# Statistics, the first query eviction and the second query product ahead of a second attention, in another order

## What is computed

```python
x = x + tanh(g_xattn[0]) * L0_xattn(_layernorm(x), ctx, ...)     # cross attention
x = x + tanh(g_ffn[0])   * L0_ffn(_layernorm(x), ...)            # 8 experts, one per token, and a shared one
x = x + tanh(g_xattn[1]) * L1_xattn(_layernorm(x), ctx, ...)     # cross attention with bias and mask
x = x + tanh(g_ffn[1])   * L1_ffn(_layernorm(x), ...)            # ReLU with LoRA, two of them
```

```python
_layernorm: (x - mean) / sqrt(var + eps)
q = (query @ w_q.T + b_q) ;  scores = (q * SCALING) @ k.T + attn_bias, masked ;  softmax
```

## Time and profile before

| | us |
|---|---|
| median of 3 runs | 190.07 |
| lowest, highest | 189.88, 190.09 |
| the profiled execution | 189.79 |
| its span, first to last instruction | 188.0 |
| TensorE busy in it | 171.0 (91%) |
| VectorE busy in it | 145.8 (78%) |
| ScalarE busy in it | 79.9 (43%) |
| GpSimd busy in it | 78.4 (42%) |

### The profile page before, as it was taken

One profiled execution on the slowest core, in us unless ns is written; L12 is line 12 of the kernel. 1 busy time (PEld: TensorE's weight loads), 2 busy tenths in 40 slices (PEclk: granted clock), 3 DMA queues, 4 the chain that ended last, 5 costly groups with the idle time before them and its releaser, 6 DMA issues.

```text
span 188.0 us, 4325 instructions
## 1 busy us (share of the span) xinstructions
PE 171.0 (91%) x1606; PEld 94.8 (50%) x1606; DVE 145.8 (78%) x364; ACT 79.9 (43%) x178; POOL 78.4 (42%) x88
## 2 busy tenths in 40 slices
PE   8768599999998979899998969989999998998994
PEld 2234236555576446366665923333555555643593
DVE  0599997889989799385666496799989996869942
ACT  3253284664473342255554002245544556255300
POOL 8729991004043864005666603255674454110000
PEclk9999969999999999999999997999999999999999
DMA  6999999940002010444421030000000000000012
GB/s 158 321 420 362 257 239 247 207 137 2 3 0 24 29 58 31 89 105 91 78 51 31 6 111 4 0 2 2 3 0 3 0 3 0 3 0 0 3 40 71
DMA packets 19558, 15.01 MB, mean 80 GB/s; under 512 B 3493, under 2 KB 18087, under 8 KB 19282
## 3 DMA queue, kind: packets, MB, share of 16 engines
q1 hardware_dynamic: 18370, 13.17, 27.9%
q0 software_dynamic: 736, 1.07, 1.8%
q10 hardware_dynamic: 432, 0.50, 1.1%
HBM read 7.82 MB, written 6.85 MB: 78 GB/s over the span
## 4 chain that ended last, share of the span: by engine, by line
PE 53%; DVE 26%; issue 7%; DMA 5%; POOL 5%; ACT 2%; SPq 0%; DVEq 0%; POOLq 0%
PE bank L877 44%; PE bank L954 6%; DMA xr<-x_in 3%; POOL rstd L311 3%; DVE oT L640 2%; DVE Sa L633 2%; DVE xn L585 2%; POOL Sx L384 2%; DVE st L566 2%; PE bank L1193 2%; DVE Vx L606 2%; DVE mx L635 2%; DMA sorted_rows<-Pe,slot 1%; DVE QT L614 1%; DMA big<-sorted_rows 1%
## 5 line engine op out<-in xcount | busy, mean ns | idle before, releaser
L877 PE MATMUL bank<-Kx,QT 128*64 128x512 f32 x128 | 34.9, 629 | 2.6 <-DVE Sx L626 2.0
L311 POOL TENSOR_TENSOR rstd<-ve,nhalf 128x2 f32<-128x2 f32 x16 | 11.7, 728 | 54.1 <-DVE ve L572 54.0
L461 ACT ACTIVATE Pe<-Sx 128x512 f32<-128x512 f32 x32 | 20.2, 630 | 27.3 <-POOL Sx L384 15.1
L954 PEld LDWEIGHTS bank<-cst,Pe 128*128 128x128 f32 x128 | 13.8, 143 | 25.1 <-issue 14.6
L372 POOL DMA_INDIRECT routed_rows<-big x15 | 14.8, 984 | 19.3 <-DVE big L842 12.2
L465 ACT ACTIVATE big<-bank 128x512 f32<-128x512 f32 x32 | 18.8, 587 | 8.5 <-PE bank L954 8.2
L954 PE MATMUL bank<-cst,Pe 128*128 128x128 f32 x128 | 21.4, 291 | 0.7 <-ACT Pe L461 0.6
L384 POOL TENSOR_TENSOR Sx<-Sa,mx 128x512 f32<-128x512 f32 x16 | 16.8, 1049 | 11.3 <-DVE mx L635 11.3
L640 DVE RECIPROCAL oT<-bank 128x128 f32<-128x128 f32 x16 | 15.3, 953 | 3.7 <-PE bank L877 3.6
L877 PE MATMUL bank<-zb 128*32 128x512 bf16 x47 | 15.5, 473 | 2.5 <-DVE bo L597 1.4
L414 ACT ACTIVATE xn<-xr,nmr,rstd 128x128 f32<-128x128 f32 x20 | 9.1, 486 | 16.0 <-DVE nmr L578 16.0
(11 more groups left out here) (110 smaller groups left out, 302.9 us busy)
## 6 DMA issues: line engine op xcount, KB each, us to landing
sorted_rows<-empty SPq DMA_DIRECT2D x1, 4686.0 KB, 29.0
wgu<-rgu SPq DMA_DIRECT2D x1, 2048.0 KB, 10.6
wdn<-rdn SPq DMA_DIRECT2D x1, 1024.0 KB, 12.6
big<-sorted_rows SPq DMA_DIRECT2D x15, 66.0 KB, 1.9
ctxT<-ctx_in SPq DMA_DIRECT2D x2, 256.0 KB, 4.7
xr<-x_in SPq DMA_DIRECT2D x2, 256.0 KB, 5.3
wf<-ffn SPq DMA_DIRECT2D x1, 512.0 KB, 4.4
Kx<-KT SPq DMA_DIRECT2D x16, 32.0 KB
```

The source lines that it names most:

```text
L311: pool.tensor_tensor(rstd[:, w], ve[:, w], nhalf[:, w], ALU.pow).then_inc(s_pow, 1)
L461: act.activation(Pe[:, u % 3, :], Sx[:, u % 2, :], ACT.Exp).then_inc(s_exp, 1)
L877: return pe.matmul(o, l, r, start=first, stop=last, **k)
L954: ins = pe.transpose(bank[2 + u % 2][:, m * P:(m + 1) * P], Pe[:, u % 3, m * P:(m + 1) * P], ident)
```

## The change

Only orders change; no instruction is new except that two `keep_warm` pairs are gone.

1. VectorE, ahead of the second attention: residual and statistics of pieces 0 and 1 come first, then the normalise of piece 0, residual and statistics of piece 2, the normalise of piece 1, Q's first eviction, residual and statistics of piece 3, the normalise of piece 2.
2. TensorE: the product of Q's piece 1 no longer stands ahead of the attention but behind the scores of unit 0, and the two pairs of `keep_warm` around it are left out.

```diff
-            for a in range(PIECES):
+            def residual2(a):
+
                 dve.wait_ge(d_yg[a], 16)
                 dve.scalar_tensor_tensor(out=xres[2][:, piece(a), :], in0=yg[:, piece(a), :], scalar=tg[:, 2:3],
                                          in1=xb[:, piece(a), :], op0=ALU.mult, op1=ALU.add).then_inc(s_res, 1)
                 dve.wait_ge(s_res, RES_X2 + a + 1)
-                if a >= 1:
-                    normalise(2, a - 1)
-                if a == 3:
-                    q_evac(1, 0)
                 stats(2, a)
+
+            for a in (0, 1):
+                residual2(a)
+            normalise(2, 0)
+            residual2(2)
+            normalise(2, 1)
+            q_evac(1, 0)
+            residual2(3)
+            normalise(2, 2)
             attention(1, ffn1_step)
...
                         if bp < PAIRS:
                             scores(layer, 2 * bp + hh)
+                        if bp == 0 and hh == 0 and layer == 1:
+                            q_proj(1, 1)
...
                 xn_transpose(2, a)
-                keep_warm(6, 2)
-                q_proj(1, a)
-                keep_warm(6, 2)
+                if a == 0:
+                    keep_warm(6, 2)
+                    q_proj(1, 0)
+                    keep_warm(6, 2)
             attention(1, ffn1_up)
```

## The result

The changed kernel takes 189.22 us (median of 20 runs, 188.23 to 189.91) against 190.03 for the kernel before beside it (20 runs, 189.01 to 191.25). The ratio is 0.9957, 95% interval 0.9937 to 0.9977: 0.8 us faster, between 0.4 and 1.2.

The account below looks back on a forecast made before the run. The prediction took the chain of waits to bound the kernel, TensorE on it for 53% of the span, VectorE 26%. Unit 2's scores coming about 1.07 us sooner, lasting to the end, gave 190.07 - 1.07 = 189.0 us, range 188.3 to 189.6.

Parts of the forecast that it names:

- 1.78 us of unused time: Q's first product, ended at 117.92, waits 1.78 us for its eviction while VectorE does residual 3 and normalise 2.

Follow-up runs that it names:

- e4: Changed kernel with keep-warm matmuls filling TensorE's idle stretches at 21.9 and 109.7 us (7, and 6 + 20 in place of 16); 187.75 us, ratio 0.9892.
- e3: Kernel before with keep-warm matmuls filling TensorE's idle stretches at 21.9 and 109.7 us (7, and 6 + 20 in place of 16); 189.43 us, ratio 0.9976.
- e1: Changed kernel with VectorE's new order alone, TensorE keeping the old one; 189.43 us, ratio 0.9966.
- e2: Changed kernel with TensorE's new order alone, VectorE keeping the old one; 191.75 us, ratio 1.0087.
- e8: Changed kernel with only the idle stretch at 109.7 us filled (6 + 20 keep-warm matmuls in place of 16); 188.49 us, ratio 0.9932.
- e7: e4 without the pair of keep-warm matmuls ahead of the transposes of piece 2; 187.79 us, ratio 0.9905.
- the first filling: 7 keep-warm matmuls in TensorE's idle stretch at 21.9 us; alone on the changed kernel 187.92 us, alone on the kernel before 189.45 us.
- e6: e4 with 24 in place of 20 keep-warm matmuls ahead of the transposes of piece 0; 189.01 us, ratio 0.9952.

## What to carry to other kernels

Slack hides not only work but chance: before, 1.78 us of unused time hid where the low clock lay, and an order that uses the slack up exposes it, so an idle stretch ahead of the new path becomes worth filling (e4 gains 1.5 us by filling two such stretches, e3 0.6, though not all of the difference is explained). Measure a small change by distances from the last instruction that it can't touch, since spans of single executions mix it with all that is ahead. Try the parts of a change alone: here one part was worth 0.9 to 1.0 of the 1.6 us, the other alone cost 1.8, and only together do they free both engines.

## What the runs showed of the hardware

- The granted clock was at its lower level in stretches of 3.4 us or twice that, and where a stretch lies differs between executions of the same instructions: for 3.4 us (before) and 6.8 us (after) from about 23.3 us on, from about 25 us on in e1, e2 and e8, and in e1, e2 and e7 also once between 11 and 15.1 us. Behind TensorE's idle 1.9 to 2.0 us between 22 and 24.3 us it fell in all five profiles without the first filling; behind the idle 1.42 or 1.43 us ahead of the 16 keep-warm matmuls in one of six (before). The statement of the Trainium skill (TensorE: Matmul & The Clock Gate, "What's actually happening") that the hardware's watch doesn't start with the kernel fits this.
- 3.4 us more of the lower level, from 26.7 us on, cost 1.5 us; a low stretch between 11 and 15.1 us cost nothing to be seen in e7; one during the keep-warm matmuls cost 0 in the old order, and its delay of the transposes, made by hand in e6, 0.7 in the new.
- 16 matmuls of 512 columns in bfloat16 took 3.63 us at a clock of 1.00 and 5.31 with 3.4 us of it at 0.51.
- A GpSimd power of two columns took 0.88 us when a residual had begun 0.18 us ahead (113.69 in the profile of before), 0.79 beside a residual that began inside it and also without one (116.73, 118.45 after), and 0.69 at 121.77 in the profile of before; VectorE's residuals took 0.48 to 0.49 throughout.
